# A graph layer with attention on one core: three value products leave the prologue for the filter stage, padding records go out between scatters, rank lookups are sent in parts

## The reference, cut to what matters

```python
xn = layernorm(x)
# graph network: per edge a record of filter values, one gathered node row, a segment sum
xs, xv = xn[:, :C] @ W_in2f_s, xn[:, C:] @ W_in2f_v          # the node table, C = 128
h = softplus(f_ij @ Wf1 + bf1) - log(2)                       # layer 1 of the filter, 20 -> 128
W = (h @ Wf2 + bf2) * rcut_ij[:, None]                        # layer 2, 128 -> 768
x_ij = products(xs[idx_j], xv[idx_j], r_ij / |r_ij|, W)
agg = segment_sum(x_ij, idx_i, num_segments=n)                # then W1, softplus, W2
# linear attention, 8 heads of 64
q, k, v = softmax(xn @ Wq), softmax(xn @ Wk), xn @ Wv
context = einsum('bhnd,bhne->bhde', k, v)
mix = einsum('bhnd,bhde->bhne', q, context) @ Wo + bo
x = x + gnn + mix
x = x + moe(layernorm(x))                                     # top 2 of 8 experts
```

## Time and profile before

| what | us |
|---|---|
| median of 3 runs (lowest, highest) | 1274.3 (1273.71, 1276.05) |
| the profiled execution | 1271.56 |
| its span | 1269.5 |
| PE busy in the span | 1190.8 (94%) |
| DVE busy | 1071.0 (84%) |
| POOL busy | 870.8 (69%) |
| ACT busy | 812.4 (64%) |

### The profile page before, as it was taken

How to read it: one execution, slowest core, us unless ns; L and a number is a source line. 1 busy time by engine, 2 the same in 40 slices (tenths; PEclk the granted TensorE clock), 3 DMA queues, 4 the chain that set the end, 5 groups by cost and what they waited for, 6 DMA issues and landing times.

```text
span 1269.5 us, 16249 instructions
## 1 busy us (share of the span) xinstructions
PE 1190.8 (94%) x4108; PEld 700.0 (55%) x4108; DVE 1071.0 (84%) x1998; ACT 812.4 (64%) x1822; POOL 870.8 (69%) x795
## 2 busy tenths in 40 slices
PE   4999999989999999899999999999999999977995
PEld 3566666767766664344444444444444444766882
DVE  5958999899989995699999999999999997589325
ACT  3667777777767660576776767767767674775330
POOL 6357777777777775688888888888888881053650
PEclk8989999999999999899999999999999999987996
DMA  9248876887799966988888898988898881554557
GB/s 276 63 153 298 296 266 256 314 304 270 291 320 358 305 236 233 351 302 309 316 309 307 305 315 305 311 309 302 315 309 304 310 265 34 203 188 143 183 172 235
DMA packets 106608, 337.65 MB, mean 266 GB/s; under 512 B 16783, under 2 KB 17803, under 8 KB 100373
## 3 DMA queue, kind: packets, MB, share of 16 engines
q0 software_dynamic: 57264, 188.75, 41.5%
q1 hardware_dynamic: 49252, 147.88, 35.4%
HBM read 211.27 MB, written 125.30 MB: 265 GB/s over the span
## 4 chain that ended last, share of the span: by engine, by line
PE 76%; DVE 12%; DMA 4%; issue 3%; ACT 2%; POOL 1%; SPq 0%; DVEq 0%; POOLq 0%; ACTq 0%
PE PS L2306 22%; PE PS L2311 22%; PE PS L2242 11%; PE PS L2431 6%; DVE RR L1587 4%; PE PS L2109 3%; PE PS L2119 2%; PE PS L2087 2%; DMA X<-in_x 1%; DMA edge_records<-RR 1%; DVE h_low L1580 1%; PE PS L2240 1%; PE PS L2409 1%; POOL edge_records L953 1%; PE PS L2202 1%
## 5 line engine op out<-in xcount | busy, mean ns | idle before, releaser
L990 POOL DMA_INDIRECT RR<-node_table,RR x322 | 445.4, 1383 | 112.2 <-issue 64.0
L1250 ACT ACTIVATE RR<-RR 128x256 f32<-128x256 f32 x966 | 394.5, 494 | 194.1 <-PE PS L2311 155.6
L953 POOL DMA_INDIRECT edge_records<-RR x316 | 315.0, 997 | 107.3 <-issue 72.7
L2306 PE MATMUL PS<-RR 128*125 128x512 f32 x644 | 291.6, 595 | 3.8 <-DVE RR L1765 3.7
L2311 PE MATMUL PS<-RR 128*125 128x512 f32 x644 | 289.6, 592 | 0.0
L2306 PEld LDWEIGHTS PS<-RR 128*125 128x125 f32 x644 | 121.0, 189 | 162.1 <-issue 144.4
L2311 PEld LDWEIGHTS PS<-RR 128*125 128x125 f32 x644 | 120.9, 188 | 155.5 <-issue 155.5
L1587 DVE TENSOR_TENSOR RR<-PS,RR 128x512 f32<-128x512 f32 x237 | 161.0, 687 | 23.4 <-PE PS L2242 22.7
L2242 PE MATMUL PS<-wf_high,h_high 128*128 128x512 f32 x316 | 148.5, 470 | 8.7 <-DVE RR L1587 8.4
L1765 DVE TENSOR_TENSOR RR<-RR 128x1536 f32<-128x1536 f32 (+1 forms) x81 | 141.0, 1741 | 0.0
L2242 PE MATMUL PS<-wf_low,h_high 128*128 128x512 f32 x316 | 125.9, 398 | 0.0
(11 more groups left out here) (354 smaller groups left out, 1799.1 us busy)
## 6 DMA issues: line engine op xcount, KB each, us to landing
RR<-edge_records SPq DMA_DIRECT2D x48, 1040.0 KB, 6.6
expert_inputs<-RR SPq DMA_DIRECT2D x8, 2313.0 KB, 17.7
RR<-edge_records SPq DMA_DIRECT2D x27, 520.0 KB, 5.1
RR<-edge_records SPq DMA_DIRECT2D x15, 780.0 KB, 5.5
RR<-in_L_ffn_beta_w SPq DMA_DIRECT2D x8, 1024.0 KB
expert_w_raw<-in_L_ffn_expert_w SPq DMA_DIRECT2D x8, 1024.0 KB, 7.0
RR<-edge_records SPq DMA_DIRECT2D x31, 260.0 KB, 5.2
edge_records<-RR POOLq DMA_INDIRECT x322, 4.3
```

What stands on the lines that cost most here:

```text
L953: g.indirect_dma_start(out=rec_dram, out_offset=place, in_=ST[:, j, :], in_offset=None).then_inc(scattered[c], 16)
L990: g.indirect_dma_start(out=GB[q % GBS][:, t, 1:5, :].rearrange("p k n -> p (k n)"), out_offset=None, in_=tab_dram, in_offset=bass.Indirect ...
L1250: last = a.activation(message_slot(q)[:, t, k:k + 5:4, :], GB[q % GBS][:, t, 0:k + 3:k + 2, :], ACT.Copy, scale=record_slot(q)[:, t, 4 * C ...
L2306: te.matmul(PS[0:NT, 2 * (r % PSS), :], OH[q % OHS][:, t, 0:NT], GB[q % GBS][:, t, 1:5, :].rearrange("p k n -> p (k n)"), start=(n == 0), ...
```

## The change

Four things.

1. The value products of tiles 7, 8 and 9 (FRONT = 7) leave the prologue. Their k-parts run as `late_value` in `beside`, at r = 5 of the periods t = 0, 1, 2, that is in steps 8, 14 and 20, in bank 6: parts 0 and 1 at j = 0, part 2 at j = 1, part 3 at j = 3. Wv's place is reused meanwhile, so SP loads Wv a second time (`WV_again`, 768 KB and 256 KB) after the table has gone out. ACT evacuates at the start of the next period, and query and context wait for it.
2. The prologue's order is rewritten on PE, ACT and DVE (bank 6 for late transposes, 7 for late table products, 4 for the bias rows, 5 for the counts): the first steps' `transposes` and `layer1` start between table products; rounded weights and the reciprocal lengths come earlier; `block_bases` stands between two `normal` calls; the rank lookups are sent in three parts (blocks 0 to 2, 3 to 5, 6 to 9) between pieces of steps 0 and 1.
3. The six padding records go out one by one after the scatters of steps 1, 3, 5, 7, 9 and 11. Constants that POOL made ahead are made behind `spare_places`.
4. SP loads feature chunk 0 ahead of Wq and Wk. The blank regions come one chunk later, and the last one stands by itself behind the loop, ahead of Wo.

```diff
+        EARLY_XT = 6
+
+        def xT_bank(t):
+
+            return t % 2 if t < EARLY_XT else 6
+
+        def table_bank(t):
+
+            return 2 if t < FRONT else 7
+
+        def value_bank(t):
+
+            return 3 + t % 2 if t < FRONT else 6
...
+        SPARE_STEPS = range(1, 1 + 2 * (NCOL - LOOPED), 2)
-        BLANK_STEP = [TILE_STEP] + [2 * CHUNK * k + 2 for k in range(1, BLANKS)]
+        BLANK_STEP = [SPARE_STEPS[-1] + 5, 27, 41, 57]
...
+            sp.wait_ge(edge_places, 2)
+            load_projection(WV_again, Wv, wqkv_in[2])
+
+            def blank_regions(n):
+                sp.wait_ge(blank_ready, n // 2 + 1)
+                blank_rows(n // 2 + BLANKS * (n % 2))
+
             sp.wait_ge(empty_ready, 1)
             for k in range(2, CHUNKS):
                 sp.wait_ge(f_staged, CHUNK * (k - 1))
                 load_features(k)
-                sp.wait_ge(blank_ready, (k - 2) // 2 + 1)
-                blank_rows((k - 2) // 2 + BLANKS * (k % 2))
+                if k > 2:
+                    blank_regions(k - 3)
...
+            blank_regions(CHUNKS - 3)
             sp.wait_ge(k_psum, NB)
             sp.dma_start(wo, Wo.rearrange("(k p) n -> p k n", p=P)).then_inc(wo_in, 16)
...
             pool.wait_ge(empty_ready, 1)
-            for n in range(NCOL - LOOPED):
-                spare_record(LOOPED + n)
             pool.wait_ge(edge_places, 2)
             for m in range(STEPS):
                 scatter(m // RING, m % RING)
+                if m in SPARE_STEPS:
+                    spare_record(LOOPED + SPARE_STEPS.index(m))
...
             def filters(i, c):
                 m = i * RING + c
                 t, r = divmod(m - TILE_STEP, PER)
+                if r == 0 and 1 <= t <= NB - FRONT:
+                    values(FRONT + t - 1)
...
+            places_in_blocks(range(0, 3))
+            hidden(0, 0)
             stage_f_low(0, 2)
-            hidden(0, 0)
+            places_in_blocks(range(3, 6))
+            low(0, 0)
+            hidden(0, 1)
+            stage_f_low(0, 3)
+            places_in_blocks(range(6, NB))
+            edge_rows()
...
+            def late_value(t, k):
+
+                if t == FRONT and k == 0:
+                    pe.wait_ge(wqkv_in[2], 64)
+                if k == 0:
+                    pe.wait_ge(qT_ready, t - FRONT + 1)
+                last = te.matmul(PS[0:NT, value_bank(t), :], XTQ[:, t, k, :], WV_again[:, k, :], start=(k == 0),
+                                 stop=(k == KD - 1))
+                if k == KD - 1:
+                    last.then_inc(v_psum, 1)
...
             def context(t):
                 pe.wait_ge(k_norm, t + 1)
+                pe.wait_ge(v_ready, t + 1)
...
-                elif 0 <= t < NB and r == PER - 1 and j == 2:
-                    context(t)
+                elif 0 <= t < NB and r == PER - 1:
+                    if j == 2:
+                        context(t)
+                    elif t < NB - FRONT:
+                        for k in ((0, 1), (2,), (), (3,))[j]:
+                            late_value(FRONT + t, k)
```

More of the change, by code:

```diff
@@ L338, in gps_layer @@
         assert c1_early <= c2.at - 2 * P and c2.at <= acc_at
-        in_hidden = 4 * 512 // RC1
-        mask_at = [hidden_at + b * RC1 if b < in_hidden else kn_at + (b - in_hidden) * RC1 for b in range(NB)]
-        assert c1_early <= hidden_at and (NB - in_hidden) * RC1 <= 3 * D
+        FRONT = 7
+        mask_at = [vn_at + FRONT * D + b * RC1 for b in range((NB - FRONT) * D // RC1)]
+        mask_at += [kn_at + b * RC1 for b in range(2 * D // RC1)]
+        mask_at += [qw_at, mi_at, spare_at]
+        assert c1_early <= hidden_at and len(mask_at) == NB and RC1 <= D and spare_at + RC1 <= r1_words
         block_mask = [R1[:, w:w + RC1] for w in mask_at]
@@ L905, in _ @@
             g.affine_select(out=two_rows, in_=ones[:, 0:P], compare_op=ALU.is_gt, fill=0.0, base=2, pattern=[[0, P]],
[L906 to L916, removed]
+                            channel_multiplier=-1).then_inc(consts, 1)
             pool.wait_ge(b2_in, 32)
@@ L1125, in _ @@
             table_rows(0)
+            act.wait_ge(nrm_sq, 1)
+            a.activation(inv, ssq, ACT.Sqrt).then_inc(nrm_root, 1)
             act.wait_ge(x_in[1], 32)
@@ new lines, in _ @@
+            table_rows(2)
+            evac_xT(3)
+            moments_of((6, 7))
+            values(2)
+            table_rows(3)
+            evac_xT(4)
+            moments_of((8, 9))
+            later_std(slice(6, NB), NB - 1)
+            a.preload_act_table_set("natural_log_exp_and_others")
+            rounded_weights()
+            stage_f(0)
+            stage_f(1)
+            values(3)
+            table_rows(4)
+            evac_xT(5)
+            values(4)
+            table_rows(5)
@@ L1168, in radial @@
+            evac_xT(6)
+            act.wait_ge(w_ordered, 2)
+            a.activation(b2hl[0:2, :], b2f, ACT.Copy).then_inc(w_rounded, 1)
             def radial(i, c):
@@ L1223, in filters @@
                     copy_qT(t)
-            bias_rows()
-            table_rows(NB - 1)
             radial(0, 0)
             stage_f(2)
-            values(NB - 2)
+            table_rows(6)
+            evac_xT(7)
             log_part(0, 0)
             radial(0, 1)
+            stage_f(3)
+            values(5)
+            table_rows(7)
+            evac_xT(8)
+            log_part(0, 1)
             high(0, 0)
-            stage_f(3)
-            values(NB - 1)
-            log_part(0, 1)
+            values(6)
             radial(0, 2)
             stage_f(4)
+            table_rows(8)
+            evac_xT(9)
+            bias_rows()
+            table_rows(9)
+            log_part(0, 2)
             radial(0, 3)
-            log_part(0, 2)
             for m in range(STEPS):
@@ L1437, in block_bases, with places_in_blocks, edge_rows @@
                 v.tensor_scalar(cpad, cpad, -1.0, None, ALU.add).then_inc(spare_bases, 1)
[L1439 to L1441 removed]
+            def places_in_blocks(blocks):
+                for b in blocks:
                     step(v.scalar_tensor_tensor(rnk, block_mask[b], off[:, b:b + 1], rnk, ALU.mult, ALU.add))
+            def edge_rows():
                 v.tensor_copy(posi[:, 0:FULL], rnk[:, 0:FULL]).then_inc(edge_places, 1)
@@ L1559, in stage @@
                     dve.wait_ge(scattered[c], i * (16 * STEP))
+                elif c == 2:
+                    dve.wait_ge(tab_psum, NB)
+                elif c == 3:
+                    for s in range(2):
+                        dve.wait_ge(tab_out[s], 32 * (NB // 2))
                 v.tensor_copy(ST[:, c * STEP:(c + 1) * STEP, 4 * C:REC], meta[:, cols, :]).then_inc(staged, 1)
```

187 lines of the change are left out of this document (99 added, 88 removed).

## The result

| | before | changed |
|---|---|---|
| median, us (lowest, highest; runs) | 1274.01 (1273.11, 1276.05; 4) | 1289.65 (1287.6, 1292.98; 4) |
| profiled execution, us (span) | 1271.56 (1269.5) | 1287.6 (1285.8) |

The ratio is 1.0129, with a 95% interval of 1.0105 to 1.0153. The changed kernel is 15.6 us slower, where 7.7 were forecast. The time lies just above the range, whose upper end was 1289.0. The direction and the place were right, the size was half of what was measured.

What follows compares the result with a forecast made beforehand. PE and POOL together were taken to bound the filter stage. On the profiled 1271.6 us, -5.0 + 12.7 + 1.0 - 1.0 = +7.7 gave 1279.3, or 1282.0 as a median; the range was 1269 to 1289.

Steps and rivals of the forecast that it cites:

- The bound and the place: Filter stage: PE and POOL must gain together, and the wait for Wo at step 64 is the term that decides.
- I take 12.7: Step 64: extra PE wait for Wo behind 2827 KB of blank rows in SP's queue, 12.7 us, bounds 10 and 18.
- Both cancel: After the stop at step 64: 1.0 us lost to a lower clock, about 1.0 given back by DVE's backlog.
- Without the rest both engines come 5 us earlier: Filter stage without the Wo stop: PE 5.1 us earlier from step 21, POOL 5.0 earlier at the stage's end.
- The start: Filter start: 10.0 us earlier through the shorter prologue, of which PE carries 9.2 into the stage.
- The late values: Steps 8, 14 and 20: products of 3.44 us each partly fill PE's idle time and cost 4.1 us in all.
- The padding records: POOL's program in the first steps: 1.27 us each, one goes into a wait, five cost 6.3 us.
- What POOL was to win back: Filter stage after step 2: POOL loses 2.1 us of later waits for its feeders.
- The ring: Rival, chance 0.07: in steps 12 to 20 DVE waits longer for landings and PE with it, costing 0 to 3 us.
- Wo is not late: Rival, chance 0.16: no longer stop at step 64, so the gains stay and the time is 1269.3 us.
- The late values are not hidden: Rival, chance 0.08: steps 8, 14 and 20 cost PE 10.3 us, 6.2 more than the forecast, giving 1288.2 us.
- A padding record costs more than a scatter: Rival, chance 0.02: each takes POOL 3.3 us instead of 1.27, six cost 12 more, giving 1294 us.

Runs made afterwards that it cites:

- Experiment 2: The kernel before, with the seventh blank region held back to step 59 so that two regions stand ahead of Wo: 1285.6 us.
- experiment 1: The changed kernel with the last blank region issued directly behind Wo instead of ahead of it: 1276.2 us.
- experiment 3: The changed kernel with the six padding records sent ahead of the first scatter again: 1282.8 us.
- experiment 4: The changed kernel with padding records and blank regions both as before the change, keeping the shorter prologue and late values: 1270.8 us.
- experiments 6 and 7: 6: the changed kernel, last blank region behind Wo and the expert matrices, 1273.4 us; 7: the same with padding records ahead of the first scatter, 1270.9 us.
- kernels 8 to 10: Built on experiment 4: last blank region behind the expert matrices, 1269.2 us; POOL's constants made ahead, 1269.0 us; both together, 1269.8 us.

## Why the prediction was right and wrong

The prediction had the mechanism right, and failed in two terms of its sum: what the extra region costs in the queue, and the lead that is left on POOL when the stop comes.

**The bound and the place: right.** PE and POOL had to gain together, and the stop at the first product with Wo decided. Experiment 2 shows the stop by itself, experiments 1 and 6 its absence.

**"I take 12.7": too small.** The stop beyond the 0.94 of before measured 14.3 us. The step that failed is the one that gave the queue all of the DMA engines, 340 GB/s, for the last 1.3 MB, since POOL would be dry and its scatters landed 9 us after PE's stop. SP's issues, and the time to landing of what was issued between 400 and 417 us (KB each, us; Wo's long issue reaches into it), show otherwise:

```profile
383.36 0.58 SPq L724 DMA_DIRECT2D expert_inputs<-RR  x1
...
387.87 1.26 SPq L725 DMA_DIRECT2D expert_inputs<-RR  x1
393.54 9.20 SPq L795 DMA_DIRECT2D RR<-in_L_mix_Wo  x1
```

```profile
RR<-in_L_mix_Wo SPq DMA_DIRECT2D x1, 1024.0 KB, 31.6
...
edge_records<-RR POOLq DMA_INDIRECT x14, 8.2
```

PE stopped at 409.9, but POOL sent scatters until 416.71, and with 8.2 us each to landing they kept moving until about 424, 14 us after PE's stop and not 9. From 420 to 424 us their queue q0 still took half of the engines, by the share at the end of each row:

```profile
q0 software_dynamic: 265, 0.87, 54.1%
q1 hardware_dynamic: 390, 0.77, 49.6%
```

So q1 kept its half nearly up to the landing. From SP's first issue of a blank region (383.36; 386.07 before) to Wo's landing (393.54 + 31.6 = 425.1; 411.7 before) the changed kernel took 41.7 us, the kernel before 25.6. The 2827 KB cost the queue 16.2 us, 175 KB per us, which is nearly the 16.8 that the rate of the earlier trace rows alone gives. The same count gives 15.6 us in experiment 2 and 17.2 in experiment 3. PE's wait grew by less than that, since SP's issues came 2.7 us earlier than before and PE reached the product with Wo only 0.8 earlier: 16.2 - 2.7 + 0.8 = 14.3. The forecast had both come earlier by the same amount. In steps 60 to 64 DVE waited four times for landings, 2.3 us in all, and PE's lead fell by 1.9.

**"Both cancel": wrong.** PE needed 6.43 us from the first product with Wo to the next bias product (425.14 to 431.57). In the kernel before it was 4.39, from 411.67 to 416.06. PE stood in neither stretch, so these 2.0 us are the clock. Windows of the changed kernel, with the granted clock third from the end:

```profile
404.00:412.00 8.00, 5.14 (x23) 3.55 (x21) 7.36 (x16) 5.03 (x10) 6.12 (x7) 1.00 1.04 365
412.00:418.00 6.00, 0.00 (x0) 0.00 (x0) 2.21 (x4) 0.00 (x0) 4.46 (x5) 0.54 1.03 336
418.00:424.00 6.00, 0.00 (x0) 0.00 (x0) 0.00 (x0) 0.00 (x0) 0.00 (x0) 0.50 1.03 408
424.00:428.00 4.00, 2.86 (x6) 1.72 (x7) 0.00 (x0) 0.32 (x1) 0.00 (x0) 0.50 0.50 191
428.00:432.00 4.00, 4.00 (x15) 2.93 (x14) 2.68 (x6) 2.08 (x5) 1.20 (x2) 0.81 0.00 0
```

The granted clock was at its lower level (0.50, 1.2 GHz) in the stop, and was not back as soon as the work was. I had put 1.0 on this, and 1.0 the other way for DVE's backlog. The backlog gave 0.6: PE waited 0.20 us for DVE in step 65 (at 432.86) where it had waited 0.75 before. On PE the stop makes 14.3 + 2.0 - 0.6 = 15.7 where 12.7 + 1.0 - 1.0 stood. On POOL it makes 16.5, in part because POOL stood a second time, 2.31 us before 444.81. For this wait the profile names no cause, and experiments 2 and 3 don't have it.

**"Without the rest both engines come 5 us earlier": wrong, POOL had 0.2 left at step 63.** The start was right in size: PE's lead at step 8 was 9.5 (changed kernel) and 10.3 (experiment 4), with 9.2 carried into the stage. The late values cost 1.9, 1.7 and 1.8 us of PE's lead (the last as read in experiment 3, where no ring wait lies beside it), 5.4 and not 4.1. I had added 0.5 to the 1.48 us of idle time in step 8 because durations overstate busy time. Without that addition a period costs 3.44 - 1.48 = 1.96, which is what step 8 measured. (Three times 3.44 - 2.0 are also 4.3 and not 4.1; and 2827 KB at 340 KB per us are 8.3 us, not 8.5.) The padding records cost POOL what they were to cost: its lead fell from 8.6 at step 3 to 2.1 at step 13, by 6.5, which is five of them. What POOL was to win back didn't come. From step 3 to step 63 POOL needed 8.5 us more than before: 6.3 for five padding records, 1.9 because its scatters were longer (1007 ns in the mean of the whole stage against 997), and 0.3 more of waiting, where 2.1 less was forecast. Most of its 3.2 us of waiting was one wait of 2.30 us for DVE at step 40 (292.19). With 8.6 instead of 9.2 at step 3, this is the whole way from the forecast's 5.0 to 0.2. Why the scatters were longer, and why DVE was late there, no experiment shows.

The ring, which I had as a rival with 0.07 and 0 to 3 us, took its part on PE. POOL was 9 to 11 us behind PE in steps 12 to 18 against 4 to 6 before, and DVE's staging waited for landings:

```profile
165.72 0.18 DVE L1615 COPY RR<-RR 128x32 f32<-128x32 f32 x1 [2.67 <-DMA edge_records<-RR]
```

These waits are 14.4 us in the whole stage, against 3.8. My reason for a low price was that POOL has scatters in hand meanwhile. That is right at the time of the wait, but PE's lead is gone for good (2.7 at step 59, 7.8 without the records in the loop), and POOL can't be earlier than PE lets it be: at step 39 both are 2.8 earlier. How much of this reached the end isn't shown, since POOL's own account above holds only the wait at step 40 that could come from it. Experiments 6 and 7 put 2.5 us on the padding records with no stop in the way, and 3 has 5.5 to 6.9 with it. In the profiled executions of 3 and of the changed kernel POOL's end differs by 4.4, and 3.9 of these are there at step 63, ahead of the stop.

**"Wo is not late": excluded** by the wait of 15.25. **"The late values are not hidden"** was half right as a mechanism: 5.4 of 10.3 us weren't. **"A padding record costs more than a scatter": excluded**, 960 ns in the mean of six, with 0.3 of idle time each.

The range missed by 0.65 us at its upper end. It was made from single mishaps, each added to the forecast alone. The wait for Wo was within its bounds of 10 and 18, while the lead on POOL was 4.8 below the forecast, more than the 0 to 3 of the ring allowed, and both came together: 16.5 - 0.2 = 16.3 where 12.7 - 5.0 = 7.7 stood.

## What to carry to other kernels

When a transfer is moved in a queue, look at what stands behind it there and when that is needed: the slack of the next item (here 0.94 us of waiting already, so none) sets the price, not the slack of the moved one. Price the moved bytes at the rate that the queue has beside its neighbours (here 175 KB per us, half of what all engines move), and count from the issue, since the neighbour's backlog outlives the engine that feeds it. A start won ahead of a long full stage is a lead that several small costs draw on, each through its own engine. Write it down per engine and step, because the engine with the least lead counts, and costs on different engines did not add here (experiments 6 and 7). A long stop of PE cost its clock as well: 2.0 us on top of 14.3.

## What was not expected of the hardware

An issue on SP took long when much was queued: Wo's took 9.20 us (rows above) against 0.38 in the kernel before, 7.00 in experiment 2 and 7.11 in experiment 3. Each of the three came behind more than 5 MB that SP had ordered in q1 in the 10 us before.

A queue that got no new work still held its share of the DMA engines while it had a backlog: q0 had 54.1% of them 3.3 to 7.3 us after POOL's last issue, with scatters that took 8.2 us to land.

The same program shows different leads in two executions. The changed kernel and that of experiment 1 are the same program up to the issues at step 59, yet POOL's lead at step 60 was -0.3 in one and -4.2 in the other, with DVE's landing waits at 14.4 and 17.7 us. So a lead that is read from one execution is uncertain by some microseconds where the ring runs near full, and this holds for the leads above too. It may be why kernels 8 to 10 could not be told apart.
